# The copies of a query and of a key tile put ahead of sines and folds in two slots of a transformer block

## The reference

```python
def _fourier_kernel(x, proj_mat):                      # D_HEAD 32, D_KMAP 128
    p = jnp.einsum('blhd,dm->blhm', x, proj_mat) / math.sqrt(D_HEAD)
    return jnp.concatenate([jnp.cos(p), jnp.sin(p)], axis=-1) / math.sqrt(D_KMAP)

q = (x @ Wq.T + bq).reshape(Bv, Lv, N_HEAD, D_HEAD)    # 16 heads; k and v alike
q_prime, k_prime = _fourier_kernel(q, proj_mat), _fourier_kernel(k, proj_mat)
kv = jnp.einsum('blhm,blhd->bhmd', k_prime, v)
out = jnp.einsum('blhm,bhmd->blhd', q_prime, kv).reshape(Bv, Lv, D_MODEL)
attn = out @ Wo.T + bo

x = _layernorm(x + attn)
x = _layernorm(x + depooled_context(x, ctx))           # rmsnorm, x @ W_in.T, a table of 64 patches
x = _layernorm(x + fp6_block_quantised(x) @ fp6_block_quantised(weight).T + bias)
return x
```

## Time and profile before

| | us |
|---|---|
| median of 3 runs | 1628.83 (1627.93 to 1632.57) |
| the profiled execution, its own time | 1629.87 |
| its span, first to last instruction | 1627.5 |
| TensorE busy | 1564.6 (96%) |
| VectorE busy | 1208.0 (74%) |
| ScalarE busy | 1113.9 (68%) |
| GpSimd busy | 715.5 (44%) |

### The profile page before, as it was taken

How to read it: one execution, slowest core, us unless ns; L and a number is a source line. 1 busy time by engine, 2 the same in 40 slices (tenths; PEclk the granted TensorE clock), 3 DMA queues, 4 the chain that set the end, 5 groups by cost and what they waited for, 6 DMA issues and landing times. The chain is left out here.

```text
span 1627.5 us, 29746 instructions
## 1 busy us (share of the span) xinstructions
PE 1564.6 (96%) x11188; PEld 1116.4 (69%) x11188; DVE 1208.0 (74%) x1849; ACT 1113.9 (68%) x1450; POOL 715.5 (44%) x633
## 2 busy tenths in 40 slices
PE   8999999999999999999999999999799999999996
PEld 6756765676676667667667766765478888888884
DVE  5687577668767766876776687898687777877876
ACT  5796677678667767867777786668256655565664
POOL 4233115203412410340232044373288978898886
PEclk9999999999999999999999999999899999999998
DMA  5100102201210220120022022001512222222211
GB/s 173 53 27 28 52 1 79 79 1 36 83 39 1 79 79 2 52 81 25 1 79 79 2 66 89 30 27 52 150 49 85 85 78 84 84 79 83 78 40 65
DMA packets 49175, 95.75 MB, mean 59 GB/s; under 512 B 3552, under 2 KB 3872, under 8 KB 49056
## 3 DMA queue, kind: packets, MB, share of 16 engines
q1 hardware_dynamic: 39776, 76.67, 15.0%
q10 hardware_dynamic: 9280, 17.31, 2.9%
HBM read 60.38 MB, written 33.59 MB: 58 GB/s over the span
## 5 line engine op out<-in xcount | busy, mean ns | idle before, releaser
L793 DVE SCALAR_TENSOR_TENSOR feat<-feat,phases 128x1024 f32<-128x1024 f32 x256 | 300.9, 1217 | 167.2 <-ACT feat L683 167.1
L683 ACT ACTIVATE feat<-phases 128x1024 f32<-128x1024 f32 x256 | 248.4, 1024 | 127.3 <-PE phases L533 108.2
L690 ACT ACTIVATE feat<-feat 128x1024 f32<-128x1024 f32 x256 | 271.7, 1062 | 74.8 <-DVE feat L793 66.0
L396 POOL TENSOR_TENSOR xt_hi<-xt_raw,singles 128x512 fp32r<-128x512 f32 x60 | 67.7, 1158 | 481.1 <-PE bank L525 451.0
L696 ACT ACTIVATE feat<-feat 128x1024 f32<-128x1024 f32 x256 | 257.2, 1046 | 8.8 <-DVE feat L800 8.4
L800 DVE TENSOR_SCALAR feat<-feat 128x1024 int32<-128x1024 int32 x256 | 209.6, 823 | 45.8 <-ACT feat L690 45.3
L418 POOL TENSOR_TENSOR res<-res,bo_all 128x512 f32<-128x512 f32 x60 | 75.5, 1283 | 211.0 <-DMA res<-x 210.7
L595 PE MATMUL kv_sum<-feat,v 128*32 128x256 f32 x2048 | 123.8, 382 | 0.0
L621 PE MATMUL kv_sum<-feat,kv_cols 128*32 128x512 f32 x1024 | 123.1, 598 | 0.0
L523 PE MATMUL bank<-xt_hi,win_hi 128*128 128x512 f32 x256 | 108.3, 423 | 7.9 <-DVE win_lo L745 7.9
L1305 ACT ACTIVATE xs<-xs,shift,rstd 128x512 f32<-128x512 f32 x96 | 71.5, 807 | 63.4 <-POOL shift L1168 63.4
(11 more groups left out here) (219 smaller groups left out, 3611.6 us busy)
## 6 DMA issues: line engine op xcount, KB each, us to landing
normed<-res SPq DMA_DIRECT2D x32, 513.0 KB, 4.2
xt_raw<-xT SPq DMA_DIRECT2D x15, 1024.0 KB, 7.3
res<-x SPq DMA_DIRECT2D x30, 512.0 KB, 4.2
xs<-normed SPq DMA_DIRECT2D x24, 513.0 KB, 3.9
out<-xs ACTq DMA_DIRECT2D x24, 512.0 KB, 2.8
feat<-normed SPq DMA_DIRECT2D x8, 513.0 KB, 3.8
out<-feat ACTq DMA_DIRECT2D x8, 512.0 KB, 2.8
xt_raw<-ctx SPq DMA_DIRECT2D x8, 256.0 KB, 3.6
```

Of the source, the lines that this page charges most:

```text
L683: act.activation(feat[2 * (w % 2) + p][:, 0, :], phases[:, 2 * p:2 * p + 2, :].rearrange("p h n -> p (h n)"), ACT.Identity, bias=ROUND).th ...
L690: act.activation(f[:, 1, :], f[:, 0, :], ACT.Sin, scale=-TWO_PI).then_inc(sin_done, 1)
L793: dve.scalar_tensor_tensor(f[:, 0, :], f[:, 0, :], ROUND, phases[:, 2 * p:2 * p + 2, :].rearrange("p h n -> p (h n)"), ALU.subtract, ALU.s ...
```

## The change

In slot 13 the step Q(1,3) stands ahead of `sin(13)`, and in slot 14 the step K(0,0) ahead of `sin(14)`:

```diff
-        13: [sin(13), Q(1, 3), cos(13), W(0, 0), W(0, 1), out(12)],
-        14: [sin(14), K(0, 0), cos(14), W(0, 2), W(0, 3), stats(0), out(13)],
+        13: [Q(1, 3), sin(13), cos(13), W(0, 0), W(0, 1), out(12)],
+        14: [K(0, 0), sin(14), cos(14), W(0, 2), W(0, 3), stats(0), out(13)],
```

## The result

The changed kernel takes 1610.44 us, the median of 6 runs (1609.64 to 1614.69), against 1631.38 for the kernel before in the same comparison (6 runs, 1627.93 to 1635.82). The ratio is 0.9875 with a 95% interval from 0.9856 to 0.9894, so 17.3 to 23.5 us less. The forecast was 1611.3 us. The profiled execution has a span of 1608.1 us, 19.4 under the one before.

The account below looks back on a forecast made before the run. The prediction took TensorE, busy 96% of the span, to bound the kernel. Removing 13.0 us of slot 13's waits and 4.5 of slot 14's, 17.5 together, from the 1628.83 us median gave 1611.3 us, range 1608 to 1617.5.

Parts of the forecast that it names:

- That only TensorE's standing still counts, and where: TensorE is 96% busy; gainable waits are 10.9 us ahead of W(0,1) in slot 13, 2.4 ahead of W(0,3) in slot 14.
- The price of a wait: In slots 13 and 14 each TensorE wait costs about 0.3 us beyond its idle field, for refilling the pipeline.
- Slot 13's reserve: With the low half ahead of the folds, W(0,1)'s bank is free 0.40 us before TensorE asks; the wait goes whole.
- rival 1: Some 0.3 us of idle stay in slot 13, seven batches keep 4.2 us with refilling: 1615.5 us; chance 0.10.
- rival 2: Gain lost from slot 15 on to GpSimd or transfers, or no effect: 1625 to 1629 us; chance 0.07.
- ScalarE's new wait: In slot 13 the high half waits 0.4 us for its product; about 2.5 of ScalarE's 4.33 us idle remain.
- Rival 3: ScalarE's wait for slot 13's product delays later roundings, phases and TensorE: about 1634 us or more; chance 0.03.
- the copies are immune: In slot 13 GpSimd stretches folds to 0.68 to 1.83 us, but the low half takes 0.74 in all 64 places.
- The rule of the Trainium skill: Counter-argument: one bias addition could delay slot 13's low half 1.3 us in six batches, making the gain some 6 us smaller.
- The size: Both waits gone in seven batches: 13.0 us in slot 13 plus 4.5 in slot 14, together 17.5 us; chance 0.80.

Follow-up runs that it names:

- The two extra instructions: Changed kernel with two more VectorE maximum instructions over the bank ahead of the low half in slot 13: 1615.32 us, ratio 0.9914.
- the run with one extra instruction: Changed kernel with one more VectorE maximum instruction over the bank ahead of the low half in slot 13: 1611.66 us, ratio 0.9898.

## Why the prediction was right, point by point

- **That only TensorE's standing still counts, and where.** Right. The seven waits for `stack_lo` ahead of W(0,1) and the seven for `keys` are gone, and nothing took their place in slots 13 to 15. The short waits elsewhere, said to stay as they were, did not quite: the three for `stack_lo` of 0.7 us together became one of 0.3, and two more with no releaser in the profile came up.
- **The price of a wait.** Right: the idle field plus 0.3 us. The forecast slot was 11.13 us, measured 11.14, and 13.0 + 4.5 us is what the two rows of seven lost. The two extra instructions showed the same surcharge from the other side. That it is the pipeline being filled again is the prediction's reading; the runs show its size alone.
- **Slot 13's reserve.** The working gave 0.40 us for batch 2; there the low half now ends at 406.34, some 0.7 us ahead of the need, because VectorE came to its fractions 0.2 us earlier in its slot. The run with one extra instruction puts the reserve at about 0.6 us. No residue stayed, so rival 1 is refuted.
- **Given back later (rival 2).** Refuted: the phases that end the seventh pass's changed slots come 18.2 us earlier than before, and the last phases of all 19.8 us earlier. No wait for `phases` or for GpSimd's split inputs came up, and GpSimd's idle time ahead of L428 is still 6.18 us.
- **ScalarE's new wait.** Right: 0.56 us, and of the 4.33 us of idle time ahead of out(12)'s copy 2.36 are left, where about 2.5 were expected. Rival 3, slower by ScalarE's order, did not occur, and not with ScalarE's half of the change alone either: slot 14 stayed at 82.4 us there, so ScalarE was not late for its roundings. That kernel was slower, by 6.8 us, on another path: the late sines delayed the low half, which still stood behind the folds, and the longer waits were followed by stretches at the lower clock.
- **GpSimd.** Right that folds held up by its additions make the waits uneven, and that the copies are immune: without the additions, slot 13 of batches 1 to 6 runs from 12.19 to 12.44 us where it ran from 12.63 to 13.55. The rule of the Trainium skill (page "SBUF — State Buffer", section "Who interferes with whom") on two SBUF inputs did not show here. L814 ran 64 times in the changed kernel as well, 16 of them beside a GpSimd instruction of 128x512, and it took 739 to 750 ns in all, with a column and a tile as its SBUF inputs. Whether that is because the column does not count as an input, no run here tells. The evidence was thinner than the prediction makes it: in the kernel before, 14 of the 64 ran beside such an instruction, and only one of them beside a bias addition; now six do.
- **What it didn't see.** It summed the two slots as if each stood for itself. The total was right only because both copies went ahead of the folds: slot 13 alone gives 8 us and not 13, since the earlier slot 14 runs into GpSimd's splits. A forecast for half of the change would have missed.
- **The size.** 17.5 us forecast, 17.5 in the changed slots of the trace, 20.9 between the medians. The interval of the ratio begins at 17.3 us. The stretches at the lower clock, which the prediction doesn't mention, explain the remainder between the two profiled executions. That the time itself came within 0.9 us of the forecast is in part luck: the gain between the medians was 3.4 us larger than forecast, but the kernel before measured 1631.38 us in the comparison and not the 1628.83 that the forecast set out from, and the two differences nearly cancel. That the kernel before loses more to them on average, because it has more long waits, fits with the two runs in which slot 13 had such stretches, but with single traces it is only argued.

## What to carry to other kernels

When an engine waits for a buffer, look at what stands ahead of the freeing instruction in the queues of the engines that free it: here a 0.74 us copy stood behind two folds that nobody needed soon. Work out the arrival of every input at the new place, on each engine of the chain, since moving the step on one of them alone gave 5.2 of slot 13's 13.0 us on VectorE, and a loss on ScalarE. And when one stall goes, the work behind it slides against the other engines' timetable, so a collision can come up in the next slot, as the seven waits for the keys did when slot 13 alone was changed; ask of each freeing instruction whether it would survive that.

## What the runs showed of the hardware

- A fold of 128x1024 on VectorE takes 0.68 to 0.70 us alone and up to 1.83 beside GpSimd's additions or splits of 128x512, while fractions of 128x1024 (1.20 to 1.22 us each) and low halves (0.74 to 0.75 us), which read PSUM and one SBUF tile, kept their durations beside them.
- Behind single waits of 1.4 to 2.4 us TensorE's granted clock was in some cases at 1.2 GHz for about 3.5 us, and matmuls of 128x512 started 0.43 us apart and not 0.23, a further 1.6 us. Behind the wait of 2.12 us in the kernel before it was not, and of three waits of 1.90 us in the run with ScalarE alone it was behind two. So a wait can cost about double its length, and not every time.
